# Routed gate and up products of an expert layer as three fp32r products of rounded parts and remainders

## What is computed

```python
shared = silu(xt @ sg_w.T) * (xt @ su_w.T) @ sd_w.T
probs = sigmoid(xt @ router_w.T + routing_bias)
topk_p, topk_idx = top_k(probs, 2)              # 2 of 8 experts, gates normalised to sum 1
g = einsum('th,eih->tei', xt, wg)               # wg, wu: (8, 256, 128)
u = einsum('th,eih->tei', xt, wu)
y = einsum('tei,ehi->teh', silu(g) * u, wd)
routed = einsum('te,teh->th', w, y)             # w: the gates, zero for experts not chosen
return shared + routed
```

## Time and profile before

| | |
|---|---|
| runs (us) | 1433.0, 1424.39, 1427.52; median 1427.52 |
| the profiled execution (us) | 1436.25, its span 1434.5, mean granted clock 0.85 |
| TensorE busy (PE) | 1031.0 us, 72% |
| VectorE, ScalarE, GpSimd busy | 693.1 us (48%), 642.5 us (45%), 454.2 us (32%) |
| stages by the trace (us) | first 0 to 137; expert layer 137 to 483; third 483 to 1080; expert layer 1080 to 1434 |

### The profile page before, as it was taken

The page is one execution under the profiler, slowest core; times in us unless marked ns, Lnnn a source line. Parts: engine busy times, 40 slices in busy tenths (PEclk is TensorE's granted clock), DMA queues, the critical chain, the costliest instruction groups (busy, mean ns, idle before and its releaser), DMA issues.

```text
span 1434.5 us, 21222 instructions
## 1 busy us (share of the span) xinstructions
PE 1031.0 (72%) x7312; PEld 607.1 (42%) x7312; DVE 693.1 (48%) x1482; ACT 642.5 (45%) x938; POOL 454.2 (32%) x529
## 2 busy tenths in 40 slices
PE   4765657875779568788878878777777786776861
PEld 2654535653555323233333333333335564544540
DVE  4885432421333244786777778775544223232311
ACT  1221322523234455777776777775333252432320
POOL 2101333134425143342333323331141404424324
PEclk9996678987899775899998999997768899878876
DMA  9300021122123444353433434311001111212322
GB/s 303 99 0 0 16 65 59 53 63 66 39 83 92 154 143 156 117 165 118 149 119 137 141 112 164 123 45 60 30 23 50 52 58 55 64 43 70 98 58 68
DMA packets 115710, 125.82 MB, mean 88 GB/s; under 512 B 9760, under 2 KB 77984, under 8 KB 115488
## 3 DMA queue, kind: packets, MB, share of 16 engines
q1 hardware_dynamic: 83104, 95.69, 20.4%
q0 software_dynamic: 8192, 16.79, 4.0%
q10 hardware_dynamic: 24320, 12.06, 2.9%
HBM read 62.39 MB, written 62.13 MB: 87 GB/s over the span
## 4 chain that ended last, share of the span: by engine, by line
PE 39%; issue 17%; another core or an unknown queue 13%; DVE 11%; DMA 8%; SPq 6%; ACT 4%; POOL 1%; ACTq 0%; POOLq 0%; DVEq 0%
PE psum L612 11%; DVE ring_b L1611 7%; PE psum L1406 5%; PE psum L639 5%; PE psum L1358 5%; DMA stacks<-stack_qr 3%; PE psum L573 2%; PE psum L623 2%; PE psum L1423 2%; SPq L1754 2%; DMA stacks<-stack_ky 2%; SPq L1749 2%; SPq L1826 2%; PE psum L588 1%
## 5 line engine op out<-in xcount | busy, mean ns | idle before, releaser
L1611 DVE TENSOR_SCALAR ring_b<-psum 128x1024 int32<-128x1024 int32 x160 | 195.7, 1223 | 145.8 <-PE psum L1358 145.7
L612 PE MATMUL psum<-w_expert,ring_a 128*128 x368 | 203.9, 680 | 67.1 <-ACT ring_a L769 60.5
L1485 ACT ACTIVATE ring_a<-psum 128x1024 f32<-128x1024 f32 x160 | 163.2, 1024 | 141.9 <-PE psum L1358 140.4
L1491 ACT ACTIVATE ring_b<-ring_b 128x1024 f32<-128x1024 f32 x160 | 168.3, 1054 | 52.6 <-DVE ring_b L1611 52.6
L1358 PE MATMUL psum<-stacks 32*128 32x128 f32 (+3 forms) x1024 | 105.6, 394 | 116.9 <-DVE ring_b L1611 89.0
L1092 DVE TENSOR_TENSOR ring_b<-psum,ring_b 128x512 f32<-128x512 f32 x96 | 64.2, 669 | 257.5 <-ACT ring_b L754 231.7
L871 POOL DMA_INDIRECT x_sorted<-r_rows,rows_of x128 | 123.7, 966 | 197.3 <-DVE rows_of L1061 161.3
L1715 POOL TENSOR_SCALAR_AFFINE_SELECT ring_b<-ring_b 128x512 f32<-128x512 f32 (+1 forms) x112 | 82.0, 746 | 309.9 <-ACT ring_b L1491 309.9
L878 POOL DMA_INDIRECT r_rows<-y_sorted,rows_of x128 | 122.3, 956 | 115.4 <-DVE x_res L1107 48.7
L1358 PEld LDWEIGHTS psum<-stacks 32*128 32x128 f32 x1024 | 61.9, 197 | 215.0 <-ACT ring_a L1485 83.3
L1603 DVE TENSOR_SCALAR ring_a<-ring_a 128x1024 f32<-128x1024 f32 x160 | 122.9, 772 | 39.5 <-ACT ring_a L1485 39.5
(11 more groups left out here) (168 smaller groups left out, 1326.3 us busy)
## 6 DMA issues: line engine op xcount, KB each, us to landing
ring_a<-x_sorted SPq DMA_DIRECT2D x40, 256.0 KB, 3.4
y_sorted<-y_out ACTq DMA_DIRECT2D x40, 256.0 KB
stack_q<-parts SPq DMA_DIRECT2D x32, 256.0 KB
stack_ky<-parts SPq DMA_DIRECT2D x32, 256.0 KB
stacks<-stack_q SPq DMA_DIRECT2D x32, 256.0 KB
stacks<-stack_ky SPq DMA_DIRECT2D x32, 256.0 KB
stack_k<-parts SPq DMA_DIRECT2D x32, 256.0 KB
stacks<-stack_k SPq DMA_DIRECT2D x32, 256.0 KB
```

Source lines behind the costliest of these rows:

```text
L612: mm = nc.tensor.matmul(bank(2 * (k % 2) + m), x_turned[:, n % 2, (i % 4) * 128:(i % 4 + 1) * 128], w["w_expert"][:, bass.ds(columns[m], 2 ...
L1485: nc.scalar.activation(exps[:, n % RING, 2 * u:2 * u + 2, :], psum[:, first:first + 2, :], ACT.Exp, scale=SCALE).then_inc(self.exp, 1)
L1491: nc.scalar.activation(part, part, ACT.Ln, bias=1.0).then_inc(self.ln, 1)
L1611: nc.vector.tensor_scalar(ring[:, m % RING, HEADS_B[u][0]:HEADS_B[u][1] + 1, :].bitcast(I32), psum[:, first:first + 2, :].bitcast(I32), 0x ...
```

## The change

1. `attn_a_pool`: the third `rstd` is computed ahead of the wait for the weights. After the fourth and each later one GpSimd splits the gate and up weights of the routed experts (two behind the fourth, one behind each of the next six): `tensor_copy` of 128x512 to fp32r into `w_high` (columns 8T to 16T of `stacks`), then a subtraction that puts the remainder in place of the weights in `w_expert`.
2. `quad_copy` rounds the turned x to fp32r; a new VectorE step, `quad_lower`, subtracts that from bank 6. What waited for `quad_copied` on TensorE (`pair_gate_up`, `quad_turn`, `turn`) waits for `quad_low`. `quad_lower` of quad 0 stands first in a group on VectorE, ahead of `vector_first`; that of quad q+1 behind `pair_hidden` of pair 2q.
3. `pair_gate_up` makes three fp32r products for each slot instead of one float32 product. Two addresses are worked out from the register of each slot; `table` holds the expert's number times 256 instead of 768, so `pair_down` multiplies it by three.
4. The third stage overwrites `w_high`. SyncE stores it to DRAM once, ahead of the first expert layer's loads, and brings it back ahead of the second's loads, when the third stage's scores are done. The second half of the first `load_a` waits for the first layer's last gate and up product.

```diff
             na.pool_rstd(p, 1)
             na.pool_rstd(p, 2)
+            na.pool_rstd(p, 3)
             p.wait_ge(loaded, 16 * len(rest_loads))
...
-            with p.Fori(1, B + 1) as b:
-                na.pool_rstd(p, b + 2)
+            for b in range(4, B + 3):
+                na.pool_rstd(p, b)
+                for e in ((0, 1) if b == 4 else (b - 3,)):
+                    if e < ROUTED:
+                        nc.gpsimd.tensor_copy(w_high[:, e], gate_ups[:, e]).then_inc(routed_high, 1)
+                        p.wait_ge(routed_high, e + 1)
+                        nc.gpsimd.tensor_tensor(gate_ups[:, e].bitcast(F32R), gate_ups[:, e], w_high[:, e].bitcast(F32),
+                                                ALU.subtract).then_inc(routed_low, 1)
...
-                pe.wait_ge(self.quad_copied, n + 1)
+                if g == 0 and j == 0:
+                    self.wait_weights(pe)
+                pe.wait_ge(self.quad_low, n + 1)
                 pe.wait_ge(self.hidden, k - 1)
                 for m, i in enumerate(pair_slots(j)):
-                    mm = nc.tensor.matmul(bank(2 * (k % 2) + m), x_turned[:, n % 2, (i % 4) * 128:(i % 4 + 1) * 128],
-                                          w["w_expert"][:, bass.ds(columns[m], 2 * INNER)], start=True, stop=True)
+                    high, low = (turned_parts[:, n % 2, part, (i % 4) * 128:(i % 4 + 1) * 128] for part in range(2))
+                    weight_high = stacks[:, bass.ds(columns[m] * 2 + (8 * T - 2 * INNER), 2 * INNER)]
+                    weight_low = w_low[:, bass.ds(columns[m] * 3, 2 * INNER)]
+                    into = bank(2 * (k % 2) + m)
+                    nc.tensor.matmul(into, high, weight_high, start=True, stop=False)
+                    nc.tensor.matmul(into, low, weight_high, start=False, stop=False)
+                    mm = nc.tensor.matmul(into, high, weight_low, start=False, stop=True)
...
-                                              w["w_expert"][:, bass.ds(columns[m] + (2 * INNER + c * D), D)],
+                                              w["w_expert"][:, bass.ds(columns[m] * 3 + (2 * INNER + c * D), D)],
...
             def sync(self, sp):
+                if self.led:
+                    self.previous.wait_scores_done(sp)
+                    sp.wait_ge(weights_kept, 16)
+                    sp.dma_start(high_flat, high_store).then_inc(weights_back, 16)
...
+            def quad_lower(self, v, g, q):
+                n, width = QUADS * g + q, min(4, SLOTS - 4 * q) * 128
+                v.wait_ge(self.quad_copied, n + 1)
+                nc.vector.tensor_tensor(turned_parts[:, n % 2, 1, 0:width], bank(6, width),
+                                        turned_parts[:, n % 2, 0, 0:width].bitcast(F32), ALU.subtract).then_inc(self.quad_low, 1)
...
+                if j % 2 == 0 and j // 2 + 1 < QUADS:
+                    self.quad_lower(v, g, j // 2 + 1)
...
                 for g in range(G):
                     b = GB * (g + 1)
+                    self.quad_lower(v, g, 0)
...
+                elif p == 1:
+                    self.previous.wait_pairs(sp)
...
+            s.wait_ge(routed_high, ROUTED)
+            s.dma_start(high_store, high_flat).then_inc(weights_kept, 16)
             ffn_1.sync(s)
```

More of the change, by code:

```diff
@@ L411, in attn_a_pool @@
                 nc.gpsimd.tensor_tensor(low, whole, high.bitcast(F32), ALU.subtract).then_inc(split_low, 1)
-            with p.Fori(1, B + 1) as b:
-                na.pool_rstd(p, b + 2)
+            for b in range(4, B + 3):
[6 more added lines that the diff above has]
+                                                ALU.subtract).then_inc(routed_low, 1)
         split_high, split_low, x_zeroed = sem("split_high"), sem("split_low"), sem("x_zeroed")
+        routed_high, routed_low, weights_kept, weights_back = (
+            sem(k) for k in ("routed_high", "routed_low", "weights_kept", "weights_back"))
         x_sorted = [nc.dram_tensor(f"x_sorted{g}", (SLOTS * 128, D), F32, kind="Internal").ap() for g in range(G)]
@@ L422, in build @@
         fetched = rows_room[:, 4 * T:8 * T].rearrange("p (r a t n) -> p r a t n", r=2, a=2, t=TT)
-        x_parts = stacks[:, 0:4 * T].rearrange("p (r a n) -> p r a n", r=2, a=2)
         slot_rows = ring_a[:, 0:4 * T].rearrange("p (r s n) -> p r s n", r=4, s=4)
-        x_turned = ring_a[:, 4 * T:6 * T].rearrange("p (r n) -> p r n", r=2)
+        both_parts = stacks[:, 0:8 * T].rearrange("p (r z a n) -> p r z a n", r=2, z=2, a=2)
+        x_parts, turned_parts = both_parts[:, :, 0], both_parts[:, :, 1]
+        w_high = stacks[:, 8 * T:16 * T].rearrange("p (e n) -> p e n", e=ROUTED)
+        routed_weights = w["w_expert"][:, 3 * INNER:].rearrange("p (e n) -> p e n", e=ROUTED)
+        gate_ups = routed_weights[:, :, 0:2 * INNER]
+        w_low = w["w_expert"][:].bitcast(F32R)
+        high_store = nc.dram_tensor("high_store", (128, ROUTED * 2 * INNER), F32, kind="Internal").ap()
+        high_flat = stacks[:, 8 * T:16 * T].bitcast(F32)
         y_out = sb("y_out", [128, 2, 4, 128])
@@ L495, in __init__ @@
                 (self.stats_done, self.mean_done, self.var_ready, self.bias_ready, self.x_low, self.logit_ready, self.chain,
-                 self.table_link, self.hidden, self.shared_x, self.first_x, self.x) = (sem(f"{name}_{k}") for k in (
-                     "stats_done", "mean_done", "var_ready", "bias_ready", "x_low", "logit_ready", "chain", "table_link", "hidden",
+                 self.table_link, self.quad_low, self.hidden, self.shared_x, self.first_x, self.x) = (sem(f"{name}_{k}") for k in (
+                     "stats_done", "mean_done", "var_ready", "bias_ready", "x_low", "logit_ready", "chain", "table_link", "quad_low", "hidden",
                      "shared_x", "first_x", "x"))
@@ L503, in __init__, with wait_pairs @@
                 self.columns = {}
+            def wait_pairs(self, eng):
+                eng.wait_ge(self.gate_up, PAIR_ITEMS[-1] + 1)
             def wait_batch(self, eng, b):
@@ L658, in tensor_shared, with wait_weights @@
                 self.shared_down(pe, b)
+            def wait_weights(self, pe):
+                if self.led:
+                    pe.wait_ge(weights_back, 16)
+                else:
+                    pe.wait_ge(routed_low, ROUTED)
             def lead_tensor(self, pe, k):
@@ L768, in quad_copy @@
                     a.wait_ge(self.gate_up, pair_item((n - 2) // QUADS, 2 * ((n - 2) % QUADS) + 1) + 1)
-                nc.scalar.copy(x_turned[:, n % 2, 0:width], bank(6, width)).then_inc(self.quad_copied, 1)
+                nc.scalar.copy(turned_parts[:, n % 2, 0, 0:width], bank(6, width)).then_inc(self.quad_copied, 1)
             def quad_evict(self, a, g, q):
```

13 lines of the change are left out of this document (8 added, 5 removed).

## The result

The changed kernel takes 1438.4 us (median of 6 runs, 1434.0 to 1441.9), the kernel before 1427.6 (6 runs, 1423.0 to 1433.0): a ratio of 1.0075, 95% interval 1.0049 to 1.0102. It is slower by 10.8 us, where 8.5 us of gain were forecast. Both the sign and the range were wrong.

A forecast was written before the change was run, and what follows sets the result against it. TensorE was taken as the engine work queues for, with holes around scatters. Terms -22.8, +11.2, +2.0, +3.0, -3.0 and +1.1 summed to -8.5 us, from 1427.52 to 1419.0 us, range 1404 to 1434.

The forecast's parts named there:

- -3.0: First stage: VectorE's wait for the third rstd goes once GpSimd computes it ahead of weights' wait and splits, 3.0 us less.
- +1.1: First stage: 16 L332 instructions each 0.07 us slower beside GpSimd's splits, 1.1 us more, bounds 0 and 18.
- rival "ports": First stage: VectorE held while GpSimd splits, costing up to its 18 us of split time; 1436 us in all, chance 0.11.
- 11.2 + 2.0: Expert layers: subtraction exposed at TensorE's 16 quad waits, 0.70 us each, 11.2 us; VectorE work queued behind it, 2.0 us.
- the scatter and the hole follow with their length unchanged: Expert groups: GpSimd's scatter and the stretch where ScalarE comes late only shift, at no added cost.
- -22.8: Gate/up products on the chain: three fp32r products replace one float32 product a slot, 22.8 us less, bounds 17.5 and 30.4.
- +3.0 for the sequencer: TensorE's added register steps make more pairs wait for instruction issue, 3 us more, bounds 0 and 11.
- 147: Gate/up product slots counted on the chain: 113 at the full clock and 34 slow, of 184 computed.
- sequencer's upper bound of the forecast: TensorE's pairs: 0.19 us more in each of 56 full-clock pairs, 11 us; as a rival 1427 us, case chance 0.20.
- A triple of 0.705 us: Gate/up: three fp32r products for a slot take 0.705 us against 0.860 for one float32 product, 0.155 us less.
- the store and load of the split weights: SyncE's 2 MB store and its load back before the second layer: covered by 15 us, so zero cost.
- the end of a hole behind a scatter: Expert groups: after ScalarE's late stretch, the quad copy still resumes 3.7 us after the scatter's last issue.

The follow-up runs named there:

- experiment 5: The changed kernel run again as it is, on the chip with late ScalarE starts: 1441.6 us, ratio 1.0071 to the kernel before.
- experiment 7: Changed kernel without VectorE's subtraction; the second product takes the rounded part again, three products a slot stay: 1420.4 us, ratio 0.9935 to the kernel before.
- experiment 8: Kernel before with only the first stage's third rstd computed ahead of the weights' wait and shared splits: 1427.4 us, ratio 0.9989.
- experiment 6: Changed kernel with each split's subtraction in four 128-column pieces and the third stage's first statistics ahead of quad 0's subtraction: 1427.2 us, ratio 0.9978.
- experiment 11: Changed kernel without column loads for pairs 1 to 11 of each group, which take pair 0's experts: 1412.2 us, ratio 0.9895 to the kernel before.
- experiment 12: Changed kernel without the third product (rounded rows by the weights' remainder), subtraction and waits kept: 1411.4 us, ratio 0.9889 to the kernel before.
- experiment 1: Changed kernel with the third stage's first statistics ahead of quad 0's subtraction, on a chip without late ScalarE starts: 1288.7 us, ratio 0.9995.
- experiment 4: Kernel before with an added VectorE wait for quad 0's copy ahead of the third stage's first statistics, chip without late ScalarE starts: 1289.6 us, ratio 0.9975.
- experiment 17: Changed kernel with TensorE's column loads for the next pair one step earlier, chip with late ScalarE starts: 1458.8 us, ratio 1.0146 to the kernel before.
- experiment 18: Changed kernel with splits moved clear of L332, statistics first, remainder's products last and earlier column loads, chip with late ScalarE starts: 1432.5 us, ratio 0.9967.
- experiment 15: Changed kernel with splits clear of L332, statistics first, remainder's products last and earlier column loads, chip without late ScalarE starts: 1275.7 us, ratio 0.9873.

## Why the prediction was wrong

The forecast was -8.5 us; measured on the same chip as experiments 5 and 7 it is +12.6 by the medians, +10.1 by the ratio. I split the miss of 21.1 us into three terms. The third is what the other two leave over, so that they add up proves nothing.

**Splits: the port.** The forecast had -3.0 and +1.1, so -1.9 at the end of the stage; it is +6.1. The -3.0 was right (3.25, experiment 8). The +1.1 was 9.4. The step that failed is the reading of rows 9 and 11: L332 took 0.50 us in rows 9, and I took that for its price beside a split. GpSimd's row there, in the kernel before, says why it was so little:

```profile
29.86 0.87 POOL L409 CAST w_shared<-w_expert 128x256 fp32r<-128x256 f32 x1 [8.01 <-DMA router_bias<-in_router_bias]
```

L332 started at 30.50, when the cast had 0.23 us left, and ended 0.27 us behind it. In the changed kernel it starts with 1.09 us of a subtraction left, and ends 0.28 us behind that. The trace before held the rule, but I read a duration from it and not what GpSimd was running and for how much longer. The rival "ports" had the place right, but its price was wrong too: it charged all of GpSimd's split time, 18 us, and needed 2.4 us a step. It is one L332 a step that meets a running subtraction, 0.94 us; the first step, where two experts' splits run, loses 2.5, and one more of 14.82 us loses 2.1. The measured 1438.4 us lies in that rival's range of 1432 to 1440 by luck: it charged 18 us where the port cost 9.4, and nothing for the two terms below. The Trainium skill ("SBUF — State Buffer", Who interferes with whom) says that whichever starts second is blocked for the whole of the other. By that rule, the trace agrees: L332 starts second and ends 0.28 us behind the subtraction, and in pieces (experiment 6) it is held for 0.13. I gave the rival 0.11 because I used the rule as a price and not as a question of who starts when. 8.0 us of the miss.

**The subtraction.** The forecast had 11.2 + 2.0; experiment 7 says 21.3 (19.4 by the ratios). The 11.2 for the bare places was near: the waits for the quad are 46.8 and 47.5 us with the subtraction and 38.8 without. What failed is "the scatter and the hole follow with their length unchanged". A hole ended 3.6 to 3.8 us after the last issue in groups 0 to 2, as said, but in the tail GpSimd's fetches come in runs of 8 or 16, and there the changed kernel loses 10 us. The late rstd is some 4 of them (experiment 6). I had listed `vector_first` and `vector_second` behind the subtraction, but not what stands behind it in the last group. The other 6 are not explained: they go without the subtraction (experiment 7), but also with it when the column loads are left out (experiment 11). 8.1 us of the miss.

**The products.** Forecast -22.8 and +3.0 for the sequencer, -19.8. Experiment 7 is 8.7 us faster than the kernel before with 6.1 us lost in the first stage, so by this remainder the products gave 14.8 (16.2 if its own trace is taken, which ends that stage at 132.23). Two parts of the term were too large. One is the count: by experiment 12 some 111 to 129 slots count and not 147, which at 0.155 us is an estimate of 17 to 20 us. The other is what a pair saves. The rows of two pairs in experiment 1:

```profile
285.40 0.49 PE L636 MATMUL psum<-stacks 128*128 x1
285.73 0.39 PE L637 MATMUL psum<-stacks 128*128 x1
285.96 0.40 PE L638 MATMUL psum<-w_expert,stacks 128*128 x1
...
286.88 0.60 PE L648 MATMUL psum<-identity,ring_b 128*128 128x128 f32 x4
287.32 1.06 PE L664 MATMUL psum<-w_expert,ring_b 128*128 x8
288.33 0.49 PE L636 MATMUL psum<-stacks 128*128 x1
```

The first product starts 0.33 us before the second where the others are 0.23 apart, and the down product is followed after 1.01 us, not 0.89. The pair takes 2.93 us and not 2.74; before it took 3.04 or 3.05 (experiment 4). The 0.19 us between is just the sequencer's upper bound of the forecast. But it doesn't hold in every pair (2.7 to 3.0), and with holes moving the loads earlier cost time (experiments 17 and 18). Without the loads, or with them earlier, most such pairs take 2.7 us (experiments 11 and 15), so the loads hold the longer ones; how they do isn't shown. 5.0 us of the miss. A triple of 0.705 us itself was nearly right: 1.48 us for two.

Right were the store and load of the split weights, which no step waited for visibly, the end of a hole behind a scatter, 48 subtractions of 0.67 us, and the third rstd.

**What stays open.** Why ScalarE comes late on one chip and not on two others; why the holes answer to the column loads (25 us less without them, 10 more with them earlier); and where 14 us come from when the kernel before does without its column loads, since its pairs stay as long. Whether the changed kernel would lose less with pauses in the fetches wasn't tried.

## What to carry to other kernels

Before work goes to GpSimd beside a VectorE that sets the pace, write down which VectorE instructions read and write SBUF only and which of GpSimd's instructions will be running when each starts; then put the work where VectorE reads PSUM or waits. Products that need a remainder go last in the sum, behind those that need only the rounded part, so the remainder's making is covered. Where an instruction with a wait is put ahead of others on an engine, list what stands behind it in every variant of the loop, the last round above all.

## What the runs showed of the hardware

- VectorE's 128x512 `tensor_scalar` from SBUF to SBUF (L332): 0.43 us alone, 1.37 if a 1.59 us subtraction of GpSimd has been running for 0.5 us when it starts, 0.56 beside the same subtraction in four pieces. Beside a cast with 0.23 us left (kernel before) and beside the subtraction it ended 0.27 to 0.28 us behind GpSimd's instruction.
- The same kernel takes 1427.5 to 1435.5 us on one chip and 1291.5 on two others. On the first, 27 to 37 of ScalarE's instructions come late, mostly by 2 to 9 us and at most by 14.2 (experiment 12). In the changed kernel's trace all 34 of them start at most 4 us behind an indirect DMA that GpSimd issues. On the others none comes late, and the issues take the same 1.26 us each.
- The column loads one step earlier in TensorE's queue did nothing to the kernel before on a chip without holes, and added 0.75% to the changed kernel on the one with them.
- A scatter of 16 issues that grew by 7.2 us made each group 11 us longer.
